# A routed expert layer: page results scattered with an addition in memory, in place of stored results, gathers and weighted sums on VectorE

## What is computed

```python
logits = x @ Wr + br                       # 32 experts
top_v, top_i = top_k(sigmoid(logits), 8)   # 8 experts for each token
w_full[token, top_i] = top_v / (sum(top_v) + 1e-9)
shared = (silu(x @ Wg_s + bg_s) * (x @ Wu_s + bu_s)) @ Wd_s + bd_s
gate, up = silu(x @ Wg[e] + bg[e]), x @ Wu[e] + bu[e]
down = (gate * up) @ Wd[e] + bd[e]
out = x1 + tanh(g_ffn) * (shared + sum_e w_full[:, e] * down[e])
```

## Time and profile before

| what | value |
|---|---|
| time, median of 3 runs | 2082.16 us (2081.37 to 2082.39) |
| the profiled execution, its own time | 2083.68 us |
| its span, first to last instruction | 2082.0 us |
| mean granted TensorE clock | 0.978 of full |
| busy: PE, DVE, ACT, POOL | 1982.1, 1610.9, 1378.0, 1180.3 us |

### The profile page before, as it was taken

The page is one execution under the profiler, slowest core; times in us unless marked ns, Lnnn a source line. Parts: engine busy times, 40 slices in busy tenths (PEclk is TensorE's granted clock), DMA queues, the critical chain, the costliest instruction groups (busy, mean ns, idle before and its releaser), DMA issues. The chain is left out here.

```text
span 2082.0 us, 44128 instructions
## 1 busy us (share of the span) xinstructions
PE 1982.1 (95%) x14690; PEld 1754.7 (84%) x14690; DVE 1610.9 (77%) x3769; ACT 1378.0 (66%) x3991; POOL 1180.3 (57%) x1286
## 2 busy tenths in 40 slices
PE   7999799999999999999997799999999999999995
PEld 7898688888888888888876688888888888888884
DVE  3432258888888888888886776669999999999996
ACT  3211177788777887777763277778777777777771
POOL 1322104777777777777776300027777777777775
PEclk9999899999999999999988899999999999999997
DMA  8654478767666666666668999999999999999998
GB/s 270 222 190 165 144 296 316 274 240 243 234 244 239 239 240 238 240 237 239 239 240 260 378 298 286 285 313 391 402 398 391 396 391 396 393 399 390 397 362 286
DMA packets 299750, 614.15 MB, mean 295 GB/s; under 512 B 55397, under 2 KB 167750, under 8 KB 299526
## 3 DMA queue, kind: packets, MB, share of 16 engines
q1 hardware_dynamic: 250374, 477.05, 64.5%
q0 software_dynamic: 49152, 134.28, 17.5%
HBM read 305.13 MB, written 306.05 MB: 294 GB/s over the span
## 5 line engine op out<-in xcount | busy, mean ns | idle before, releaser
L1653 POOL DMA_INDIRECT parts<-results_dram,kept_index x512 | 518.7, 1013 | 383.9 <-DMA results_dram<-y 220.0
L837 POOL DMA_INDIRECT pages_dram<-rows,kept_index x512 | 529.6, 1034 | 198.8 <-issue 143.2
L895 ACT ACTIVATE exps<-sim,minus_max 128x78 f32<-128x78 f32 x1024 | 316.1, 349 | 14.7 <-DVE minus_max L988 14.7
L1674 ACT ACTIVATE w_h<-w_raw 128x768 fp32r<-128x768 f32 x159 | 134.1, 843 | 158.7 <-DMA w_raw<-in_experts 157.9
L895 ACT ACTIVATION_READ_ACCUMULATOR exps<-sim,minus_max 128x1 f32 x1024 | 236.2, 231 | 0.0
L1762 DVE SCALAR_TENSOR_TENSOR parts<-parts,kept_weight 128x256 f32<-128x256 f32 x448 | 213.4, 476 | 1.6 <-DMA parts<-dense_dram 0.5
L1859 PE MATMUL xps<-ident,xin 128*128 128x128 f32 x1272 | 167.1, 275 | 19.2 <-DVE wq_l L1724 7.7
L1736 DVE TENSOR_TENSOR w_l<-w_raw,w_h 128x768 fp32r<-128x768 f32 x159 | 151.6, 954 | 41.8 <-ACT w_h L1674 41.7
L141 PE MATMUL yps<-w_h,hid_h 128*128 128x256 f32 x636 | 179.6, 282 | 1.5 <-DVE hid_l L1819 1.0
L143 PE MATMUL yps<-w_l,hid_h 128*128 128x256 f32 x636 | 178.5, 281 | 0.0
L142 PE MATMUL yps<-w_h,hid_l 128*128 128x256 f32 x636 | 178.3, 280 | 0.0
(11 more groups left out here) (243 smaller groups left out, 6026.3 us busy)
## 6 DMA issues: line engine op xcount, KB each, us to landing
xin<-pages_dram SPq DMA_DIRECT2D x159, 512.0 KB, 10.9
results_dram<-y SPq DMA_DIRECT2D x159, 512.0 KB, 9.7
w_raw<-in_experts SPq DMA_DIRECT2D x159, 385.0 KB, 10.0
pages_dram<-blank SPq DMA_DIRECT2D x108, 512.0 KB
pages_dram<-blank SPq DMA_DIRECT2D x12, 1536.0 KB
keys_dram<-keys SPq DMA_DIRECT2D x16, 624.0 KB, 4.4
kT<-keys_dram SPq DMA_DIRECT2D x32, 312.0 KB
v<-values_dram SPq DMA_DIRECT2D x32, 308.0 KB
```

What stands on the lines that cost most here:

```text
L837: pool.indirect_dma_start(dram["pages"], bass.IndirectOffsetOnAxis(ap=kept_index[:, at:at + 1].bitcast(U32), axis=0), buffer(batch)[:, k / ...
L895: last = act.activation(exps[u % 2][:, h, :], scores(u)[:, h // 4, h % 4, :], ACT.Exp, bias=minus_max[u][:, h:h + 1], accum_out=row_sum[u] ...
L1653: pool.indirect_dma_start(parts[slot(batch, t)][:, k, :], None, done, bass.IndirectOffsetOnAxis(ap=kept_index[:, at:at + 1].bitcast(U32), ...
```

## The change

- A page row grows from 256 to 289 numbers (1,156 bytes): the row, the 32 weights of its token, and the token's number as an integer (`ROW`, `OF_ROW`, `TOKEN`). The zero rows of a page carry numbers of 512 spare rows behind the tokens. `scale_weights` writes the weights straight into the row buffer, and one small copy adds the token number. Both move up by one step, into the same step as `kept_index` and ahead of it.
- `match`, `weigh`, `sum_weights`, the gathers, the weighted additions, the tile stores, the results in memory and the x1 loads of the dense rounds go. The eviction of a dense round is a plain copy.
- For each page DVE reads the owner into a register (`value_load`) and makes two small copies from `xin`: the owner's weight of the 512 rows (`row_weight`) and their token numbers (`row_token`), 8 buffers each (`MARKS`).
- The eviction of a page multiplies by the weight: ACT does the first two blocks of 128 x 256, DVE the last two.
- POOL issues four indirect DMAs with addition per page, each of 128 rows of 1 KB from `y` into memory: even pages into `x1`, odd ones into `sums`. Before page p it waits until the four of page p-2 have landed. `y` is free again when they have.
- `sums` (8 MB) and the spare rows of `x1` are set to zero by 18 DMAs of 512 KB in steps 4 to 21 of the attention.
- Once all pages that can hold a token block are added, SP loads x1, sums and the dense result for it (12 blocks of 512 tokens); DVE adds them with four operations of 128 x 512 and SP stores the block. For the 4 late blocks x1 and sums are loaded only after the last page has been added, and DVE makes two additions of 128 x 1024 each.

```diff
+ROW = D + ROUTED + 1
+MARKS = 8
+SETTLED = 5
 def gpsimd(pool):
-        for batch in range(B):
-            last_round = EARLY + opened_pages(batch) - 1
-            done = dram["results"][0:opened_pages(batch) * PAGE, :]
-            for s in range(DEPTH):
-                pool.wait_ge(stored[s], 16 * ((last_round - s) // DEPTH + 1))
-            for t in range(TT):
-                if batch >= 2:
-                    pool.wait_ge(combined[t], batch - 1)
-                for k in range(TOPK):
-                    at = (batch * TT + t) * TOPK + k
-                    pool.indirect_dma_start(parts[slot(batch, t)][:, k, :], None, done,
-                                            bass.IndirectOffsetOnAxis(ap=kept_index[:, at:at + 1].bitcast(U32), axis=0)
-                                            ).then_inc(parts_loaded[slot(batch, t)], 16)
+        for page in range(OPENED):
+            n, into = EARLY + page, dram[("x1", "sums")[page % 2]]
+            if page >= 2:
+                pool.wait_ge(added[(n - 2) % DEPTH], pages_added(page - 2)[(n - 2) % DEPTH])
+            pool.wait_ge(act_out, page + 1)
+            for q in range(PQ):
+                if q == PQ // 2:
+                    pool.wait_ge(dve_out, n + 1)
+                pool.indirect_dma_start(into, bass.IndirectOffsetOnAxis(ap=row_token[page % MARKS][:, q:q + 1].bitcast(U32), axis=0),
+                                        y[n % DEPTH][:, q, :], None, compute_op=ALU.add).then_inc(added[n % DEPTH], 16)
 def scalar(act):
-            act.wait_ge(stored[s], 16 * turn)
-            for q in range(0, PQ, 2):
-                act.wait_ge(down_full, 2 * m + 1 + q // 2)
-                last = act.activation(y[s][:, q:q + 2, :], yps[:, q:q + 2, :], ACT.Copy)
+            act.wait_ge(marked, page + 1)
+            result_tile_free(act, m)
+            act.wait_ge(down_full, 2 * m + 1)
+            for q in range(PQ // 2):
+                last = act.activation(y[s][:, q, :], yps[:, q, :], ACT.Identity, bias=nothing[:, 0:1], scale=row_weight[page % MARKS][:, q:q + 1])
 def vector(dve):
+        def mark(turn, s):
+            page = page_of(turn, s)
+            dve.wait_ge(rows_loaded[s], 16 * (turn - first_turn + 1))
+            if page == 0:
+                dve.wait_ge(owner_ready, 1)
+            if page >= MARKS:
+                dve.wait_ge(added[s], pages_added(page - MARKS)[s])
+            e = dve.value_load(owner_row[0:1, bass.ds(page, 1)], min_val=0, max_val=ROUTED - 1)
+            dve.tensor_copy(row_weight[page % MARKS][:, :].unsqueeze(2), xin[s][:, :, OF_ROW][:, :, bass.ds(e, 1)])
+            dve.tensor_copy(row_token[page % MARKS][:, :], xin[s][:, :, TOKEN].bitcast(I32)).then_inc(marked, 1)
         def evict(turn, s):
+                for q in range(PQ // 2, PQ):
+                    last = dve.tensor_scalar(y[s][:, q, :], yps[:, q, :], row_weight[page % MARKS][:, q:q + 1], None, ALU.mult)
+        def sum_terms(tokens, i):
+            half = slice(i % 2 * 2, i % 2 * 2 + 2)
+            first, second = term[tokens % 2]
+            if i == 0:
+                dve.wait_ge(terms_loaded[tokens % 2], 16 * 3 * (tokens // 2 + 1))
+            if i >= 2:
+                dve.wait_ge(summed, 4 * tokens + i - 1)
+            dve.tensor_tensor(first[:, half, :], first[:, half, :], (second if i < 2 else dense_term)[:, half, :], ALU.add).then_inc(summed, 1)
         def step(turn, s):
-            if exists(turn, s, -2) and is_dense(*moved_by(turn, s, -2)):
+            if exists(turn, s, -2):
                 evict(*moved_by(turn, s, -2))
 def sync(sp):
+        def load_late_terms(i):
+            if i == 0:
+                for s, count in enumerate(pages_added(OPENED - 1)):
+                    sp.wait_ge(added[s], count)
...
+            spare = term[i // 2][i % 2]
+            for tile, rows_of in zip((xin[i][:, :, 0:D], spare[:, :, :]), parts_of_sum):
+                sp.dma_start(tile, rows_of[LATE[i]]).then_inc(late_loaded[i], 16)
```

More of the change, by code:

```diff
@@ L1211, in step @@
                         route(part, b, par, h)
+                if name == "Q3" and routes:
+                    pick_weights(b - 2)
+                    scale_weights(b - 2)
                 if (name == "T1a" and b >= B) or (name in ("T3a", "PV1b") and b == B):
@@ L1489, in rounds, with pages_added, last_page_of, final_round @@
         for n in range(first, ROUNDS):
-            turn, s = n // DEPTH, n % DEPTH
-            step(turn, s, turn - LAG if LAG <= turn else None)
+            step(n // DEPTH, n % DEPTH)
             yield
-    def is_zero(batch):
-        return isinstance(batch, int) and batch == 0
-    def slot(batch, t):
-        return TT * (batch % 2) + t
-    def x1_rows(turn, s):
-        return xin[s][:, :, 0:D] if is_late(turn, s) else parts[s // 2][:, PQ * (s % 2):PQ * (s % 2 + 1), :]
+    def pages_added(page):
+        return [4 * 16 * len(range(s, page + 1, DEPTH)) for s in range(DEPTH)]
+    def last_page_of(tokens):
+        return opened_pages(BATCHES * (tokens + 1) - 1) - 1
+    def final_round(tokens):
+        return EARLY + last_page_of(tokens) + SETTLED
+    def result_tile_free(eng, n):
+        before, s = n - DEPTH, n % DEPTH
+        if before < 0:
+            return
+        if before < EARLY:
+            eng.wait_ge(stored[s], 16 * (before // DEPTH + 1))
+        else:
+            eng.wait_ge(added[s], pages_added(before - EARLY)[s])
     def sync(sp):
@@ L1635, in sync @@
+        for i in range(2):
+            sp.wait_ge(out_stored[i], 16 * (EARLY // 2))
         for s in range(DEPTH):
-            sp.wait_ge(stored[s], 16 * len(range(s, ROUNDS, DEPTH)))
+            sp.wait_ge(stored[s], 16 * DENSE // DEPTH)
     def gpsimd(pool):
@@ L1780, in find_owners, with sum_late @@
+        def sum_late(i):
+            n = EARLY + OPENED + i
+            whole = y[n % DEPTH][:, :, :]
+            dve.wait_ge(dve_out, n + 1)
+            dve.wait_ge(late_loaded[i], 32)
+            dve.tensor_tensor(whole, whole, xin[i][:, :, 0:D], ALU.add).then_inc(late_added, 1)
+            dve.wait_ge(late_added, i + 1)
+            dve.tensor_tensor(whole, whole, term[i // 2][i % 2][:, :, :], ALU.add).then_inc(late_summed, 1)
         def find_owners(i):
@@ L1814, in step @@
                                      op0=ALU.add, op1=ALU.mult).then_inc(hidden_ready, 1)
-            sum_next(batch, s, 3)
+            for tokens in range(EARLY):
+                if final_round(tokens) + 2 <= n < final_round(tokens) + 6:
+                    sum_terms(tokens, n - final_round(tokens) - 2)
             if exists(turn, s, 2) and not is_dense(*moved_by(turn, s, 2)):
@@ L1934, in layer @@
         opened_by = sb("opened_by", [P, B * ROUTED])
-        rows = [sb(f"rows{i}", [P, TT, D]) for i in range(BUFFERS)]
-        kept = Kept(sb("kept_index", [P, B * TT * TOPK], I32), sb("kept_weight", [P, B * TT * TOPK]), sb("of_key", [P, TT, TOPK, ROUTED]),
-                    *(across.enter_context(nc.semaphore(n)) for n in ("kept_weighed", "kept_summed")))
+        rows = [sb(f"rows{i}", [P, TT, ROW]) for i in range(BUFFERS)]
         ahead = {"shared_split": [sb(f"shared_{s}", [P, EW], F32R) for s in "hl"],
```

325 lines of the change are left out of this document (122 added, 203 removed).

## The result

The changed kernel takes 2431.18 us, the median of 4 runs (2426.36 to 2435.78), against 2082.27 us for the kernel before (4 runs): a ratio of 1.167, 95% interval 1.165 to 1.170. It is 16.7% slower. I had predicted 2141 us, at most 2290: the side was right, the size was not, and the time lies outside the range.

What follows compares the result with a forecast made beforehand. PE, busy 95% of the span, was taken to bound the kernel before; after the change, landings would pace the pages: 1208 + 907.9 (5.71 us a page) + 6.1 + 19.2 = 2141 us, 2.8% slower, range 2050 to 2290 us.

Steps and rivals of the forecast that it cites:

- POOL's issue of a scatter: Page rounds: an adding scatter takes 0.95 us to issue, like a plain one; upper end 0.47 us more.
- the dear case: Page rounds, rival: the addition's read is dear in landing (2391 us) or in issue (2380 us); chance 0.20.
- the likeliest case: Page rounds: landing with a read sets the pace, 5.5 to 6.5 us a page, 2107 to 2262 us; chance 0.40.
- The attention: Attention stage: no change charged; it should end as before, near 1100 us.
- The dense rounds: Dense rounds: DVE loses x1's wait and 2 us of matching; 0 to -5 us, taken as 0.
- POOL before PE: Page rounds: four issues, some stretched by `w_l`, make POOL 5.36 us a page against PE's 5.07.
- The plain case: Page rounds, rival: the addition costs as a plain scatter; 2059 to 2106 us, 2084 at 5.36 us a page; chance 0.25.
- The landing: Page rounds: page p waits for page p-2; landing of 5.9 us plus 1.5 for the read, 5.71 us a page.
- The bytes: Page rounds: 1.67 MB a page, 4.2 us at 395 GB/s; 2.19 MB and 5.55 us if the destination's read counts.
- DVE: Page rounds: DVE's work grows from 3.5 to 5.2 to 5.6 us a page, leaving no slack.
- The end: After the last scatter lands: 8 loads, two additions and a store take 19.2 us.
- What would show it: Trace signs: scatter length, POOL's wait on page p-2, landing 7.4 us, PE gaps about 0.6 us a page, GB/s near 395 or 300.

Runs made afterwards that it cites:

- experiment 1: The changed kernel with its four scatters per page writing rows without the addition: 2079.69 us, ratio 0.9985 to the kernel before.
- Experiment 8: The kernel before the change, without the x1 loads and additions of its 12 early dense rounds: 2072.10 us.
- experiment 10: The changed kernel, additions kept, with the low part of the weights made by scalar_tensor_tensor in place of tensor_tensor: 2433.93 us.
- experiment 2: The changed kernel issuing only the first and third of a page's four adding scatters: 2029.58 us, ratio 0.9745 to the kernel before.
- experiment 12: The changed kernel with one more load of an expert's weights per page, into a tile nobody reads: 2426.99 us.

## Why the prediction was wrong

**The step that failed** is a mis-sized term of the sum, POOL's issue of a scatter: "I keep the issue at 0.95, by the two rows that agree." It measured 1.55. The two rows, gathers and plain scatters, were both of DMAs without arithmetic, so their agreement told nothing of the one with it. Even my upper end, +0.47, was short of the 0.60 that came. Four of them a page are 4 x 0.59 = 2.36 us, less 0.17 because fewer issues meet `w_l` at the slower pace (5.38 - 5.04 = 0.34 us of stretch in experiment 1, 0.17 here): 2.2 us a page and 351 us in all, the distance between experiment 1 and the result. I had given the dear case 0.20, at 2380 us, and cut it from the range. That the kernel is slower, as forecast, is no merit of the likeliest case: its pace-setter, the landing, never holds POOL up, and with the issue at 0.96 us as I had it the time is that of the kernel before (experiment 1).

**The attention**: nothing charged, and right. From 300 to 1060 us PE is busy 755.96 us after and 755.97 before, while the DMAs went from 248 to 283 GB/s.

**The dense rounds**: taken as 0 out of 0 to -5 us, measured -12.5 (-9 to -14 over the variants). I counted DVE's wait for x1 and the matching, and not the 6 MB and the 12 places in SP's queue. Experiment 8 removes the wait, the bytes and the places together, so it doesn't tell which was worth the rest.

**POOL before PE**: right. The plain case was given as 5.36 us a page and 2084 us; experiment 1 shows 5.38 and 2080. (The pace is the real match; the first page comes 12 us earlier than I had it, and its profiled execution, 2075.5 us, is nearer to that.) That POOL is slower than PE "before any price for the addition is set" held, and so did the size of the stretch, though it depends on the order and not on meeting alone.

**The landing**: my likeliest case made it the pace, 5.71 us a page. It isn't. L stood for the landing of a page's last scatter from its start, and I took 5.9 and 1.5 for the read. Of the pages between 1420 and 2000 us whose landing the trace records in full (74 here, 86 in experiment 1), the last scatter lands a median of 5.9 us after its start with the addition and 5.9 without: the read doesn't show in it. The chain is then (3 x 1.855 + 5.9) / 2 = 5.7 us a page, my own figure, but by luck, since the spacing was too short and the landing too long. Next to POOL's 7.59 us of issuing it never binds. The landing isn't a constant: listed over all four scatters it is 4.9 us here, 6.3 in experiment 10 at the same load, 7.2 and 7.0 in experiments 2 and 12.

**The bytes**: the table of queues counts no second read. Plain and adding, the software queue moves 159.19 MB:

```profile
q0 software_dynamic: 55104, 159.19, 20.7%
```

```profile
q0 software_dynamic: 116160, 159.19, 34.2%
```

The first line is experiment 1, the second the changed kernel (packets, MB, share). Of these packets 512 x 48 = 24576 belong to the attention; the rest over 636 scatters is 48 each without the addition and 144 with it. Between 1420 and 2000 us the queue holds the DMAs for 1.35 us a page without and 3.77 with the addition (24.5% of 580 us over 105.5 pages, 49.5% over 76.25). So the Trainium skill's warning in "Collectives: The Full Stack", The bandwidth ceiling, that the addition takes a second source read, points the right way for the packets' time, which more than doubles. It sets no time here (experiment 12).

**DVE**: 5.2 to 5.6 us a page, "no slack". Too much: in experiment 2 all its page work takes 524.28 us in 580 / 5.06 = 115 pages, 4.6 us. The evictions took 0.88 us as estimated; the additions and copies overlap and the register load on DVE took 0.31 and 0.19 us.

**The end**: 19.2 us after the last landing, measured 19.5.

**A reading**: the chain in the earlier trace rows holds five kinds of DVE work, with `up_ps`, not four; nothing was worked out from the count.

**What would show it**: I had asked for the scatters' length first, and it gave the answer. PE's gaps are there, with the eviction as releaser, but they are (580 - 449) / 76.25 = 1.7 us a page and not 0.6. Of the other signs, a wait of POOL for page p-2 never appears, and GB/s is 229, below both values that I had named, because the pace fell.

No complete version beat the kernel before: the shorter times all leave something out. Fewer scatters that each carry more rows were not tried; this kernel's indices go one to a partition, 128 to a DMA.

## What to carry to other kernels

Price an operation that no row shows by a run or by a wide bound, not by its nearest relative: two rows that agree about plain transfers say nothing of one that computes on the way. Where one engine issues every transfer of a stage, multiply issue time by count before thinking of bytes or landings, and to tell an issue bound from a bandwidth bound, halve the bytes and add a load: if neither moves the time, it isn't bandwidth, and an engine whose issues stand end to end names the issue. When reading a landing from a trace, check against a wait from which end of the issue it counts and which DMA of a group it belongs to.

## What the runs showed of the hardware

- An indirect DMA of GpSimd with addition costs 1.55 us to issue for 128 rows (1.25 us and 2.3 ns a row), a plain one 0.96 us (0.83 us and 1.0 ns a row), the same for rows of 512 and of 1,024 bytes in the adding case; 0.30 us lie between two of them.
- The adding one makes 144 packets for the plain one's 48, but its landing isn't longer: 5.9 us from the start of the issue for the last of a page, with and without the addition.
- An issue that starts while DVE reads two SBUF operands is longer by the time that is left until 0.12 us before DVE is done, in both DVE forms tried (`tensor_tensor`, `scalar_tensor_tensor`); one that starts first isn't touched (98 of 99 issues, and 45 of 45).
- The DMA share passed from 0.98 to 1.06 and the rate from 229 to 280 GB/s with no loss of time: a share near 1 is no proof of full DMAs.
